# Layer 0 of a two-layer graph kernel on one core: source keys through DRAM instead of by broadcast transposes, two more one-hot tiles for two fewer gathers, and the ranks cut into pieces

## The chip, the cores and the metric

The kernel runs on one core of one Trainium2 chip. The metric is the device time of the whole kernel in microseconds (us), the median of several runs. TensorE is called PE here, VectorE DVE, ScalarE ACT, GpSimd POOL and SyncE SP, as the profile does.

## The reference, cut to what matters

There are 12,500 nodes with 32 features and 400,000 edges, sorted by `dst`. Two layers are applied to `x`:

```python
h = relu(layernorm(x))                                   # layer 0
agg = segment_sum((h * node_vec1)[src], dst)             # gather by src, add by dst
x = x + agg * node_vec1_n2
h = relu(layernorm(x))                                   # layer 1
m = relu(h[src] + edge_attr_32)
x = x + (1 + eps) * h + segment_sum(m, dst)
```

All of the change that matters lies in layer 0, the first line pair with its gather by `src`.

## The kernel before

The edges are cut into 125 units of 128 x 25 edges, and these into 25 batches of five units: three "sorted" and two "plain". A batch covers a narrow range of `dst`, so its sums go into a window of PSUM by products with one-hots of the destination. What differs is how the source rows are fetched.

**Sorted units.** DVE works out for each of their edges a place in a table of records that is ordered by source (`rank_within`, `rank_sums`, `rank_places`). POOL scatters the edges there, one indirect DMA of 128 edges at a time, 75 for a batch. A batch's records then come back in one load (`load_record`), as 100 tiles of 128 edges in ten groups, the source key of each edge in column `2 * F` of its record. For each group PE turns the keys of ten tiles into rows, each by a transpose of a column broadcast to 125 partitions (`turn_keys`), ACT copies them from PSUM to `key_row` in two pieces (`copy_keys`), DVE compares them with the partition's number (`src_onehots`), and PE multiplies these one-hots with the node table held in SBUF (`pick`). DVE also makes the one-hots of the destination (`dst_onehots`), and PE adds the messages by them (`products`). This is called the sorted phase of a batch here.

**Plain units.** Their 50 tiles (one from each column) are sorted by source inside each row. Of them, `DIRECTS` = 2 * `SIDE` = 38 are picked by PE from the node table with wide one-hots, in eight steps (`CUTS`, `STEPS`), the node table being met in 20 groups of which a tile needs 3 to 8 (`SPANS`); the remaining 12 (`MID`) are gathered by POOL (`gather_mid`). The eight steps are called the wide phase here, and their steps are numbered 0 to 7. In it, DVE makes the wide one-hots of a step (`wide_onehots`), the sorting of later rows (`sort_some`) and the destinations' one-hots (`direct_onehots`); ACT copies each picked tile masked (`copy_wide`); PE picks (`pick_wide`) and adds (`direct_products`).

**Order.** Each engine has its own hand-written program, in batches, and they meet by semaphores. In the step of batch b, DVE does the rest of the sorted phase of b, then the wide phase of b. Inside or after that wide phase it ranks batch b + 2 (whose scatter POOL begins when `ranked` says so), and then begins the sorted phase of b + 1 with `first_onehots`: the source one-hots of groups 0 and 1, then the destination one-hots of these groups. PE turns the keys of the first two groups of b + 1 in the last tiles of the wide phase of b, as soon as that batch's record is loaded. SP issues all plain loads and stores in program order: a wait in its program holds back everything behind it. The PE, ACT and POOL programs loop over two batches (`over_batches`), those of DVE and SP over four in layer 0 (`over_fours`).

## Time and profile before

| | |
|---|---|
| time, median of 3 runs | 4801.34 us (4799.08 to 4803.71) |
| time of the profiled execution | 4791.23 us |
| its span, first to last instruction | 4789.2 us |
| granted PE clock over it | 0.914 |
| busy: PE, DVE, ACT, POOL | 3721.2, 3812.7, 3261.3, 3497.5 us |

The profile is of one execution. Layer 0 is the time from the start to about 3,060 us, when the last sums are added and x is loaded again, and layer 1 is the rest. Start times are counted from the first instruction. A row of the timeline merges neighbouring instructions of a line, and in brackets it gives the idle time of the engine before them and what ended it.

### The profile page before, as it was taken

The page shows a single profiled execution, that of the slowest core. Times are in us where ns is not written, and L with a number is a line of the kernel's source. Part 1 is how long each engine was busy: PE and PEld are TensorE (multiplying, and loading weights), DVE is VectorE, ACT ScalarE, POOL GpSimd, SP SyncE. Part 2 cuts the span into 40 slices and gives each one's busy share as a digit, 9 for nine tenths or more (in the row PEclk, how much of TensorE's full clock was granted, in tenths as well). Part 3 has the DMA queues.
Part 4 walks back from the last instruction along what each step waited for, and adds up shares of the span by engine and source line. Part 5 has one row for each costly group of instructions (what it writes and reads, how often), then busy time and mean ns, then how long its engine had stood idle before and what let it go on. Part 6 is the DMA issues. An engine that isn't in the chain of part 4 may idle for free.

```text
span 4789.2 us, 130194 instructions
## 1 busy us (share of the span) xinstructions
PE 3721.2 (78%) x43852; PEld 2888.9 (60%) x43852; DVE 3812.7 (80%) x11454; ACT 3261.3 (68%) x9090; POOL 3497.5 (73%) x3590
## 2 busy tenths in 40 slices
PE   0388888888888888888888899467767777777775
PEld 0266666666666666666666666356666666666664
DVE  9788888888888888888888886767777776777775
ACT  1377777777777777777777777456666766666664
POOL 6757777777777777777777777477777777777774
PEclk9999999999999999999999999778888888888887
DMA  6322222222222222222222221211212221211221
GB/s 111 63 51 54 57 54 54 54 56 54 54 54 56 54 53 54 56 54 53 54 56 54 53 54 44 72 39 54 57 43 54 57 57 54 58 49 48 57 57 26
DMA packets 439702, 262.77 MB, mean 55 GB/s; under 512 B 334660, under 2 KB 423732, under 8 KB 432632
## 3 DMA queue, kind: packets, MB, share of 16 engines
q1 hardware_dynamic: 322488, 187.55, 16.7%
q0 software_dynamic: 110816, 60.69, 6.7%
q8 instruction: 394, 6.46, 0.6%
q10 hardware_dynamic: 5728, 5.82, 0.5%
q14 instruction: 276, 2.26, 0.2%
HBM read 172.96 MB, written 80.85 MB: 53 GB/s over the span
## 4 chain that ended last, share of the span: by engine, by line
PE 32%; POOL 23%; DVE 19%; issue 13%; ACT 10%; DMA 2%; DVEq 1%; ACTq 0%; SPq 0%; POOLq 0%
POOL stage L759 22%; PE candidates L1247 18%; PE plain_ps L1259 7%; DVE arena L1753 7%; ACT message L987 5%; DVE arena L1729 4%; ACT centered L956 2%; PE sorted_agg L1187 2%; PE candidates L1157 1%; ACT arena L880 1%; POOL message L759 1%; PE key_rows L1230 1%; DMA stage<-in_edge_attr 1%; DVE counts L1475 1%; PE key_rows L1139 1%
## 5 line engine op out<-in xcount | busy, mean ns | idle before, releaser
L771 POOL DMA_INDIRECT records<-stage,place_i x1875 | 1879.0, 1002 | 696.2 <-issue 652.0
L759 POOL DMA_INDIRECT stage<-table,src_plain x1250 | 1246.9, 997 | 409.1 <-issue 377.3
L987 ACT ACTIVATE message<-candidates,member_is 128x96 bf16<-128x96 f32 x4560 | 1170.7, 377 | 429.4 <-PE candidates L1247 426.3
L1753 DVE TENSOR_SCALAR arena<-window_iota,dst_rel 128x224 bf16<-128x224 f16 (+1 forms) x4800 | 1091.2, 302 | 37.8
L880 ACT ACTIVATE arena<-key_rows 125x640 f16<-125x640 f16 x1000 | 653.2, 716 | 215.1 <-DVE arena L1729 83.2
L1187 PE MATMUL sorted_agg<-arena 128*96 128x224 bf16 (+1 forms) x5000 | 654.1, 285 | 161.0 <-DVE arena L1753 109.6
L1259 PE MATMUL plain_ps<-summed,message 128*96 128x224 bf16 x4560 | 609.2, 269 | 68.2 <-ACT message L987 68.2
L1187 PEld LDWEIGHTS sorted_agg<-arena 128*96 128x96 bf16 x5000 | 543.7, 137 | 186.1 <-issue 118.6
L1259 PEld LDWEIGHTS plain_ps<-summed,message 128*96 128x96 bf16 x4560 | 490.7, 128 | 269.6 <-ACT message L987 127.4
L1729 DVE TENSOR_SCALAR arena<-arena,row_key 125x1280 bf16<-125x1280 f16 x1000 | 554.7, 555 | 96.5 <-ACT arena L880 64.6
L1139 PE MATMUL key_rows<-ident,record 128*125 128x128 f16 x5000 | 425.8, 235 | 239.2 <-DMA record<-records 96.2
L1139 PEld LDWEIGHTS key_rows<-ident,record 128*125 128x125 f16 x5000 | 378.5, 149 | 285.9 <-issue 148.3
L1165 PE MATMUL candidates<-record,ident 128*128 128x320 f32 x500 | 240.0, 568 | 389.8 <-DVE arena L1729 389.3
L1247 PE MATMUL candidates<-parts,xs 125*128 125x480 bf16 x2304 | 526.1, 366 | 0.0
L1170 PEld LDWEIGHTS candidates<-parts,arena 125*128 125x128 bf16 x15000 | 427.0, 99 | 85.4 <-issue 70.9
L1247 PE MATMUL candidates<-parts,record 125*128 125x480 bf16 x1992 | 457.4, 367 | 0.0
L1170 PE MATMUL candidates<-parts,arena 125*128 125x32 bf16 x15000 | 425.8, 180 | 0.0
L1039 ACT ACTIVATE centered<-window_iota,plain_key 128x128 bf16<-128x128 f16 x1250 | 379.9, 391 | 26.3 <-DVE plain_key L1792 25.7
L752 POOL DMA_INDIRECT message<-table,mid_src x288 | 306.4, 1064 | 93.2 <-issue 93.2
L896 ACT ACTIVATE arena<-candidates 128x320 bf16<-128x320 f32 x250 | 108.5, 434 | 368.2 <-PE sorted_agg L1187 363.4
L888 ACT ACTIVATE arena<-candidates 128x480 bf16<-128x480 f32 x500 | 264.6, 584 | 134.0 <-PE candidates L1157 133.3
L1247 PE MATMUL candidates<-parts,arena 125*128 125x480 bf16 x1512 | 341.9, 366 | 0.0
(228 smaller groups left out, 5139.0 us busy)
## 6 DMA issues: line engine op xcount, KB each, us to landing
record<-records SPq DMA_DIRECT2D x50, 1650.0 KB
stage<-in_edge_attr SPq DMA_DIRECT2D x125, 400.0 KB, 3.2
records<-pad SPq DMA_DIRECT2D x25, 1650.0 KB, 11.9
records<-stage,place_i POOLq DMA_INDIRECT x1875
stage<-table,src_plain POOLq DMA_INDIRECT x1250
message<-table,mid_src POOLq DMA_INDIRECT x288
xs<-in_x SPq DMA_DIRECT2D x8, 390.6 KB
table<-parts ACTq DMA_DIRECT2D x4, 585.9 KB
```

The source lines that it names most:

```text
L759: pool.indirect_dma_start(message[:, k, j, :] if l == 0 else rows[:, k, j, :], None, table0 if l == 0 else table1, bass.IndirectOffsetOnAx ...
L771: pool.indirect_dma_start(records, bass.IndirectOffsetOnAxis(ap=place_i[:, h, e:e + 1], axis=0), stage[:, h, e, :], None).then_inc(scatter ...
L880: nc.scalar.activation(key_row[:, g % 2, k * HALF * P:(k + 1) * HALF * P], key_rows[k][0:NP, 0:HALF * P], ACT.Copy).then_inc(key_rows_copi ...
L987: last = nc.scalar.activation(direct_message[n % DB][:, m * WIDE:(m + 1) * WIDE], candidates[n % 2][:, m * WIDE:(m + 1) * WIDE], ACT.Copy, ...
L1039: last = nc.scalar.activation(plain_onehot[:, k, j, :], window_iota[:, 0:WS], ACT.Abs, bias=plain_key[:, k, j:j + 1], scale=-1.0)
L1139: last = nc.tensor.transpose(key_rows[k][0:NP, t * P:(t + 1) * P], column, ident16[:])
L1170: last = nc.tensor.matmul(candidates[g % 2][:, tile * F:(tile + 1) * F], src_onehot[:, g % 2, o, tile * P:(tile + 1) * P], parts[:, 2 * bu ...
L1187: last = nc.tensor.matmul(into, sorted_message[:, (2 * h + g) % MESSAGES, t, :], dst_onehot(g, t), start=(g == 0 and t == 0), stop=(g == G ...
L1247: last = nc.tensor.matmul(candidates[n % 2][:, 0:MEMBERS * WIDE], wide_onehot(s, w)[:, i * P:(i + 1) * P], parts[:, w * MEMBERS:(w + 1) * ...
L1259: last = nc.tensor.matmul(pair_agg, direct_message[n % DB][:, m * WIDE:(m + 1) * WIDE], direct_onehot[:, n % DO, :], start=(n == 0 and m = ...
L1729: nc.vector.tensor_scalar(src_onehot[:, g % 2, o, :], key_row[:, g % 2, :], row_key[0:NP, o:o + 1], None, ALU.is_equal).then_inc(src_oneho ...
L1753: last = nc.vector.tensor_scalar(dst_onehot(g, t), window_iota[:, 0:WA if tile == 0 else WT], dst_rel[:, h, tile:tile + 1], None, ALU.is_e ...
```

## The change

It has four parts, all in layer 0. (Some semaphores of the far path are merged as well, which has no part in a run on these inputs, since that path is only taken when an edge lies outside its window.)

- **Keys.** PE turns the keys of a whole batch by one transpose, 128 x 100 to 100 x 128 (`turn_all`), ACT copies it to SBUF (`copy_turned`), SP stores it to a DRAM tensor `turned`, waits for that, and loads it back group by group, 1280 keys broadcast to 125 partitions, into four buffers (`key_of`); from the fifth group on a load waits until the one-hots four groups before it are made. These stand in SP's program between the record's load and the loads of the stage and the filling of batch b + 2. `copy_keys` and `turn_keys` are gone from layer 0.
- **Tiles.** `SIDE` goes from 19 to 20: 40 of 50 plain tiles are made by one-hots, 10 gathered. Steps 3 and 4 have five tiles instead of four.
- **Ranks.** `rank_within` is cut in two: `rank_buckets` in step 2 of the wide phase and a third of the scans (`rank_scans`) in each of steps 2, 3 and 4, instead of everything at step 5.
- **Places.** `rank_sums` and `rank_places` move from behind the wide phase to the end of step 6, ahead of the one-hots of step 7; PE's `prefixes` moves from step 6 to step 5.

```diff
-    SIDE = 19
+    SIDE = 20
-    CUTS = (0, 5, 10, 15, 19)
+    CUTS = (0, 5, 10, 15, 20)
+    turned = nc.dram_tensor("turned", (BATCHES, TILES * P), F16, kind="Internal").ap()
+        def key_of(l, g):
+            return more_rows[:, g % 2, :] if l == 0 and g % KEY_ROOMS >= 2 else key_row[:, g % 2, :]
...
@@ SP, step0, behind load_record(0, b, 0)
+                if is_first(b):
+                    sp_at_least(parts_ready, CHUNKS)
+                sp.wait_ge(key_rows_copied[0], b + 1)
+                sp.sem_inc(loads_begun, 1)
+                sp.dma_start(turned_t[bass.ds(b, 1), :, :].rearrange("o t e -> (o t) e"), keys_turned[:]).then_inc(keys_stored, 16)
+                sp.wait_ge(keys_stored, 16 * (b + 1))
+                sp.sem_inc(loads_begun, 1)
+                for g in range(GROUPS):
+                    nth = GROUPS * b + g
+                    if g == 0:
+                        sp_at_least(src_onehot_ready[0], 2 * GROUPS * b)
+                    elif g >= KEY_ROOMS:
+                        sp_at_least(src_onehot_ready[0], 2 * (nth - KEY_ROOMS + 1))
+                    sp.dma_start(key_of(0, g), turned_g[bass.ds(nth, 1), :].to_broadcast([NP, GE])).then_inc(keys_loaded[g % KEY_ROOMS], 16)
                 if left >= 2:
                     load_stage(b + 2, h)
                     fill(b + 2, h)
@@ ACT
+                def copy_turned(b):
+                    act.wait_ge(key_rows_ready[0], b + 1)
+                    at_least(act, keys_stored, 16 * b)
+                    nc.scalar.activation(keys_turned[:], key_rows[0][0:TILES, 0:P], ACT.Copy).then_inc(key_rows_copied[0], 1)
...
-                            if n in (DIRECTS - 3, DIRECTS - 2):
-                                copy_keys(*after(b, h, u), n - (DIRECTS - 3))
+                            if n == DIRECTS - 3:
+                                copy_turned(b + 1)
@@ PE
+                def turn_all(b):
+                    pe.wait_ge(record_loaded[0][0], 16 * (b + 1))
+                    at_least(pe, direct_copied_keys, SUBS * b)
+                    nc.tensor.transpose(key_rows[0][0:TILES, 0:P], record16[:, 0, :, 2 * F], ident16[:]).then_inc(key_rows_ready[0], 1)
...
-                            if n in (DIRECTS - 3, DIRECTS - 2):
-                                turn_keys(*after(b, h, u), n - (DIRECTS - 3))
+                            if n == DIRECTS - 3:
+                                turn_all(b + 1)
@@ DVE, step0, at the end of step s of the wide phase
-                            if s == SUBS - 3 and more:
-                                rank_within(b + 2, h, u + 1)
-                        if more:
-                            rank_sums(b + 2)
-                            rank_places(b + 2, h, u + 1)
+                            if s == 2 and more:
+                                rank_buckets(b + 2, h, u + 1)
+                            if s in (2, 3, 4) and more:
+                                rank_scans(b + 2, s - 2)
+                            if s == SUBS - 2 and more:
+                                rank_sums(b + 2)
+                                rank_places(b + 2, h, u + 1)
                         first_onehots(*after(b, h, u))
```

How the end of a wide phase and the start of the next sorted phase stand in DVE's program, before (`record<-direct_row` is step 6, `xs<-direct_row` step 7, `summed` their destination one-hots, `counts` the rank sums, `key<-unhandled` the last of the places, and the row of line 1729 the source one-hots of groups 0 and 1):

```order
L1808 TENSOR_SCALAR record<-direct_row,wide_key 125x640 x8
...
L1819 TENSOR_SCALAR summed<-window_iota,pair_dst 128x224 x5
L1808 TENSOR_SCALAR xs<-direct_row,wide_key 125x640 x5
L1819 TENSOR_SCALAR summed<-window_iota,pair_dst 128x224 x5
L1475 TENSOR_TENSOR counts<-counts,misc 128x1250 x3
L1478 TENSOR_TENSOR counts<-counts,in_bucket 128x3750
...
L1516 TENSOR_SCALAR key<-unhandled 128x75
L1729 TENSOR_SCALAR arena<-arena,row_key 125x1280 x4
L1742 CAST dst_rel<-record 128x100
```

And of the change:

```order
L1853 TENSOR_SCALAR record<-direct_row,wide_key 125x640 x8
...
L1864 TENSOR_SCALAR summed<-window_iota,pair_dst 128x224 x5
L1516 TENSOR_TENSOR counts<-counts,misc 128x1250 x3
L1519 TENSOR_TENSOR counts<-counts,in_bucket 128x3750
...
L1557 TENSOR_SCALAR key<-unhandled 128x75
L1853 TENSOR_SCALAR xs<-direct_row,wide_key 125x640 x5
L1864 TENSOR_SCALAR summed<-window_iota,pair_dst 128x224 x5
L1774 TENSOR_SCALAR arena<-arena,row_key 125x1280 x4
L1787 CAST dst_rel<-record 128x100
```

The rank sums and places now stand ahead of step 7's one-hots, so that nothing but two short rows lies between step 7's one-hots and the source one-hots of the next batch.

SP's program between the record's load and the stage's, of the change, with its waits (`turned` is the DRAM tensor of the turned keys, `arena` and `centered` hold the four buffers; the six later loads follow as the last two rows do, each with a wait for the one-hots):

```order
L603 DMA record<-records 128x3300
L650 ISA [waits key_rows_copied0]
L650 DMA turned<-keys_turned 100x128
L651 REGISTER_ALU
L586 REGISTER_ALU [waits keys_stored]
L659 ISA [waits src_onehot_ready0]
L659 DMA arena<-turned 125x1280
L659 ISA
L659 DMA arena<-turned 125x1280
L659 ISA
L659 DMA centered<-turned 125x1280
```

Before, the record's load was followed at once by the stage's:

```order
L594 DMA record<-records 128x3300
L586 ISA
L586 DMA stage<-in_edge_attr 128x25x32
L586 ISA
L586 DMA stage<-in_edge_attr 128x25x32
L586 ISA
L586 DMA stage<-in_edge_attr 128x25x32
```

So a store, a wait for it and ten loads of 125 x 1280 keys now lie in SP's program ahead of the stage's loads.

## Rows read from the trace of the kernel before

**Rows 1.** POOL's groups of lines from 1162.37 to 2107.21 us, eight batches

```profile
L771 POOL DMA_INDIRECT records<-stage,place_i x600 | 600.2, 1000 | 213.8 <-issue 209.4 <-DVE key L1516 4.4
L752 POOL DMA_INDIRECT message<-table,mid_src x96 | 102.2, 1064 | 29.3 <-issue 29.3
```

**Rows 2.** DVE's timeline: wide phases of batches 2, 9, 10, 11, 22 begin

```profile
454.05 1.09 DVE L1808 TENSOR_SCALAR record<-direct_row,wide_key 125x640 bf16<-125x640 f16 x3
...
1277.19 1.33 DVE L1808 TENSOR_SCALAR record<-direct_row,wide_key 125x640 bf16<-125x640 f16 x3
...
1397.86 1.24 DVE L1808 TENSOR_SCALAR record<-direct_row,wide_key 125x640 bf16<-125x640 f16 x3
...
1514.83 0.67 DVE L1808 TENSOR_SCALAR record<-direct_row,wide_key 125x640 bf16<-125x640 f16 x2
...
2810.01 1.15 DVE L1808 TENSOR_SCALAR record<-direct_row,wide_key 125x640 bf16<-125x640 f16 x3
```

**Rows 3.** DVE's timeline behind the wide phase of batch 9

```profile
1355.43 1.14 DVE L1729 TENSOR_SCALAR arena<-arena,row_key 125x1280 bf16<-125x1280 f16 x2
...
1368.35 1.14 DVE L1729 TENSOR_SCALAR arena<-arena,row_key 125x1280 bf16<-125x1280 f16 x2 [4.47 <-ACT arena L880]
1371.05 1.15 DVE L1729 TENSOR_SCALAR arena<-arena,row_key 125x1280 bf16<-125x1280 f16 x2 [1.55 <-ACT arena L880]
```

**Rows 4.** DVE's timeline in and behind the wide phase of batch 10

```profile
1431.45 3.49 DVE L1808 TENSOR_SCALAR xs<-direct_row,wide_key 125x640 bf16<-125x640 f16 x9 [1.96 <-ACT direct_row L949]
...
1460.49 1.81 DVE L1808 TENSOR_SCALAR xs<-direct_row,wide_key 125x640 bf16<-125x640 f16 x5
1462.33 1.28 DVE L1819 TENSOR_SCALAR summed<-window_iota,pair_dst 128x224 bf16<-128x224 f16 x5
...
1478.13 1.14 DVE L1729 TENSOR_SCALAR arena<-arena,row_key 125x1280 bf16<-125x1280 f16 x2
...
1488.03 1.14 DVE L1729 TENSOR_SCALAR arena<-arena,row_key 125x1280 bf16<-125x1280 f16 x2 [0.52 <-ACT arena L880]
```

**Rows 5.** DVE's groups by shape, 1162.37 to 2107.21 us

```profile
L1819 DVE TENSOR_SCALAR summed<-window_iota,pair_dst 128x224 bf16<-128x224 f16 x304 | 79.5, 311 | 20.0 <-PE plain_ps L1259 4.5 <-DVE member_is L1711 1.9 <-issue 0.4
...
L1808 DVE TENSOR_SCALAR record<-direct_row,wide_key 125x640 bf16<-125x640 f16 x105 | 38.1, 400 | 1.4
...
L1808 DVE TENSOR_SCALAR record<-direct_row,wide_key 125x512 bf16<-125x512 f16 x72 | 24.1, 371 | 1.1
```

**Rows 6.** PE's timeline, a full tile and the end of the wide phase

```profile
1366.03 1.22 PE L1139 MATMUL key_rows<-ident,record 128*125 128x128 f16 x9 [4.49 <-issue]
...
1425.54 1.79 PE L1247 MATMUL candidates<-parts,xs 125*128 125x480 bf16 x8
...
1427.64 1.58 PE L1247 MATMUL candidates<-parts,xs 125*128 125x480 bf16 x7
...
1467.98 1.18 PE L1247 MATMUL candidates<-parts,xs 125*128 125x480 bf16 x5
...
1471.84 0.34 PE L1139 MATMUL key_rows<-ident,record 128*125 128x128 f16 x3
...
1479.52 0.70 PE L1157 MATMUL candidates<-parts,arena 125*128 125x96 bf16 x7 [3.87 <-DVE arena L1729]
```

**Rows 7.** SP's timeline: a store, a load behind its landing

```profile
1459.19 0.38 SPq L647 DMA_DIRECT2D ordered<-row_order  x1
1461.13 0.40 SPq L650 DMA_DIRECT2D row_order<-ordered  x1
```

**Rows 8.** ACT's timeline: first keys copied

```profile
1473.17 1.32 ACT L880 ACTIVATE arena<-key_rows 125x640 f16<-125x640 f16 x2
```

**Rows 9.** DMA issues of the page: KB each, us to landing

```profile
stage<-in_edge_attr SPq DMA_DIRECT2D x125, 400.0 KB, 3.2
```

**Rows 10.** Windows: the last two numbers are DMA share and GB/s

```profile
2989.00:2990.00 1.00, 1.00 (x9) 0.58 (x8) 0.00 (x0) 1.00 (x5) 0.94 (x1) 1.00 1.00 422
...
3104.00:3105.00 1.00, 0.00 (x0) 0.00 (x0) 1.00 (x2) 0.00 (x0) 0.00 (x0) 0.50 0.32 128
```

More of the change, by code:

```diff
@@ L401, in gnn_two_layers @@
         key_rows_copied = per_layer("key_rows_copied")
+        keys_stored = sem("keys_stored")
+        keys_loaded = [sem(f"keys_loaded_{k}") for k in range(KEY_ROOMS)]
         src_onehot_ready = per_layer("src_onehot_ready")
@@ L1429, in rank_within, with rank_buckets @@
             def rank_within(b, h, u):
+                rank_buckets(b, h, u)
+                for v in range(SORTED):
+                    rank_scans(b, v)
+            def rank_buckets(b, h, u):
                 nth = [0]
@@ L1449, in rank_within, with rank_scans, step @@
                         bucket16[:, v * J:(v + 1) * J].unsqueeze(1).to_broadcast([P, BUCKETS, J]), ALU.is_equal))
[L1450 to L1457 removed]
+                assert nth[0] == 8 + SORTED
+            def rank_scans(b, v):
+                nth = [8 + SORTED + v * len(SCANS)]
+                def step(ins):
+                    nth[0] += 1
+                    ins.then_inc(rank1_steps, 1)
+                    dve.wait_ge(rank1_steps, b * RANK1 + nth[0])
+                for some in SCANS:
+                    last = nc.vector.tensor_tensor_scan(counts[:, v, some], goes_on[:, 0:some.stop - some.start],
+                                                        in_bucket[:, v, some], 0.0, ALU.mult, ALU.add)
+                    if v < SORTED - 1 or some != SCANS[-1]:
+                        step(last)
+                if v == SORTED - 1:
+                    last.then_inc(scans_ready, 1)
+                    assert nth[0] == RANK1
             HALVINGS = []
```

59 lines of the change are left out of this document (26 added, 33 removed).

## Prediction

> **What bounds the kernel now.** The change touches layer 0 alone, so I read the groups of lines of eight batches first, to see which engine is always occupied, and then the timelines of DVE and PE over one wide phase and what follows it.
>
> POOL looks like the bound and is nearly so. A scatter takes 1.00 us and the next starts 0.30 us later, so the 75 of a batch are 97.9 us, and the 12 gathers are (102.2 + 29.3) / 8 = 16.4 us: 114.3 us in each batch [rows 1]. The batches take longer than that: DVE starts the wide phase of batch 2 at 454.05 and that of batch 22 at 2810.01, which is 117.8 us each [rows 2]. POOL waits the difference, for the ranks. So the cycle is made by DVE and PE.
>
> That cycle has two parts, cut at the first source one-hots of the next batch (called src0 below). In batch 9, W, the start of the wide phase, is at 1277.19, src0 at 1355.43 (W + 78.2), and the next W 42.4 us later. In batch 10: W at 1397.86, src0 at 1478.13 (W + 80.3), and the next W 36.7 us later [rows 2 to 4]. The sum over the two is 237.6 us. In the wide phase PE and DVE run side by side. PE starts step 7 at W + 70.1 and turns the next keys at W + 74.0; then it waits 3.87 us for src0, because DVE is still in the ranks [rows 6]. In the sorted phase DVE runs with hardly a gap in batch 10 (0.52 us for keys), while in batch 9 it waits 4.47 + 1.55 us for them [rows 3, 4], which comes from a pause of 4.49 us on PE that nothing in the profile explains [rows 6]; it comes at every second batch, where PE's program starts its loop again. So the keys' transposes and copies are beside the path in one batch of two.
>
> **What is taken off.** (1) Ninety-nine transposes and nineteen copies of a batch. In the sorted phase DVE does the same one-hots as before, so all that can be won is its wait for keys: 0.5 us in batch 10. In batch 9 the 6.0 us shrink: groups 2's keys no longer come through PE, but group 3's one-hots still wait for the second pick, which stands behind PE's pause. Counting from src0: the first pick and four products end at 6.1 as before (1366.03 - 4.49 - 1355.43), the pause at 10.6, the pick some 1.5 later, and DVE would be ready for group 3 at about 11 (1488.03 - 0.52 - 1478.13, and 1.4 of (7)); some 1.5 us stay. So 4.5 us are won there. (2) Two gathers: POOL's floor falls by 2.7 to 111.6 us, worth nothing while it isn't the bound. (3) Ranks in pieces: DVE does the same work at other moments. At step 5 it waited 1.96 us for its keys because it was ahead of PE [rows 4]; with the ranks earlier it won't be. That is 2.0 us less on DVE's way to src0 (I use it for both batches).
>
> **What is added.** (4) Two tiles that need 8 node groups each. From one 8-group tile to the next PE takes 2.10 us [rows 6], so 4.2 us, less 0.2 for two gathered tiles: PE reaches step 7 at W + 74.1. DVE gets two more destination one-hots of 79.5 / 304 = 0.26 us and 18 wide one-hots widened from 512 to 640, by 0.363 - 0.335 = 0.03 us each [rows 5]: 1.0 us.
>
> (5) Places sooner. The 1.85 us and 1.28 us of step 7 [rows 4] now come behind the ranks. DVE would start step 7 at W + 80.3 - 2.0 - 3.1 + 1.0 = W + 76.2 in batch 10, with the first pair of one-hots 0.75 us later (two of five in 1.81) at 76.9; in batch 9 at 74.9. PE wants them at 74.1, so PE now waits 0.8 to 2.8 us at step 7, which it never did. What POOL gains (its scatter may start some 3 us sooner) it doesn't need.
>
> (6) The new way of the keys, which is the main cost. PE turns them behind the third tile of step 7, 3.86 us after its start (1471.84 - 1467.98, [rows 6]), and 0.3 more because the first tile has to wait for its last one-hots: W + 81.1 in batch 10, 79.1 in batch 9. From there to src0:
> - ACT's copy began 1.33 us after the turn's start [rows 6, 8], as it finishes a tile first; with a copy of 0.3 us: 1.6. SP's reaction: 0.2.
> - The store, and the wait for it. The nearest pair, also a store to DRAM whose landing lets a load go, takes 1461.13 - 1459.19 = 1.94 us [rows 7].
> - The load. A load of 400 KB lands in 3.2 us [rows 9]. Data at full speed moves at 422 GB/s with a DMA share of 1.00; so 1.0 us of it is data and 2.2 us are fixed. But a transfer on 125 partitions, the store of the node table, runs at a share of 0.32 and 128 GB/s [rows 10]: five engines of sixteen. The key load writes 125 x 2560 B = 320 KB on 125 partitions, so 2.5 us, and lands after 4.7 us.
>
> In sum 8.4 us, all of it on the path: DVE has nothing left in its program between step 7 and src0 that could cover it, and from W + 79 on it is idle. Before, the keys were turned and copied while DVE was in 14.5 us of ranks. src0 comes at 81.1 + 8.4 = W + 89.5 in batch 10 and W + 87.5 in batch 9, that is 9.2 us later in both.
>
> (7) The second key load lands 2.5 us behind the first and DVE wants it after 1.1: 1.4 us more. Later groups are wanted every 3.4 us ((1514.83 - 1488.03) / 8, [rows 2, 4]), so a load of 2.5 us keeps ahead, with four buffers.
>
> (8) SP issues the stage's loads some 20 us later than now, behind the key loads. The scatter wants them almost a whole batch later. No cost; were the cover gone, it would be some microseconds of POOL's, which has 5 to spare.
>
> [...]
>
> **Sum.** Batch 10: + 9.2 - 0.5 + 1.4. Batch 9: + 9.2 - 4.5 + 1.4. Together 16.2 us, 8.1 a batch; there are 24 such passages: 194 us. The start adds nothing (DVE is sorting while the first keys travel). The profiled execution took 4791.2 with a span of 4789.2, so 4985; it was 10.1 us below the median of the runs shown, so I expect 4995.
>
> **Bounds.** The keys' way is between 6.4 (3.2 us for the load, ACT free at once) and 11 us (a receipt and load twice as slow to start); PE's wait at step 7 between 0 and 3; the retained part of the pause between 0 and 6. That is 5 to 11 us a batch.
>
> **Rivals.**
> - *All sixteen engines carry the keys.* Nothing in the trace shows a broadcast read from DRAM on 125 partitions. At 422 GB/s 320 KB take 0.8 us: src0 1.7 us earlier, no second wait: 8.1 - 3.1 = 5.0 us a batch, 4921. Against it is the share of 0.32 [rows 10]. With all shades up to 6 us: chance 0.22.
> - *The broadcast reads are slow*, 125 reads of the same 2560 B. At half the speed a load takes 5 us, more than the 3.4 us in which DVE uses one up. The first keys come 2.5 us later, and the tenth load lands 45 us behind the first where DVE wants it about 31 us after src0: 2.5 + 14 more, 24 us a batch, about 5380. It turns from a few us to this at 3.4 us a load. Chance 0.06, and 0.10 for something between.
> - *The keys are there before DVE wants them* (faster). Then DVE's own work sets the pace: 2.0 less and 1.0 more in the wide phase, 0.5 and 4.5 us fewer waits in the sorted one: 3.5 us a batch, from the pair's 118.8 down to 115.3, above POOL's 111.6: 4717. It decides where the way from the turn to src0 is under 2 us. The store and its wait alone took 1.94. Or PE's and ACT's lighter load shortens the wide phase by more than I see. Chance 0.05.
> - *Nothing changes*, because POOL sets the pace: against it are 3.5 us a batch of waiting. Chance 0.02.
> - My forecast, 6 to 10 us a batch: 0.55.
>
> Differences under 0.2%, some 10 us, are what a measurement of this kernel can't tell from none. The range 4895 to 5085 leaves out the ends of both sides.
>
> **What would show it.** DVE's row of the source one-hots at the head of each batch has an idle time of 8 to 11 us, ended by a DMA of `turned`; the second one has 1 to 2 us; the store and the first load stand some 2 us apart in SP's rows; the loads run at a share near 0.31; PE waits for DVE's `xs` one-hots at step 7; POOL waits 9 to 12 us a batch for ranks; the period is 125 to 127 us. Wrong would be a short wait there, which would mean the keys' way costs under 5 us, or sorted phases longer than 40 us with waits at every group, which would be slow loads.

## The result and the profile after

The changed kernel takes 5037.8 us (median of four runs, 5032.0 to 5040.0) beside 4802.3 for the kernel before (four runs, 4799.1 to 4803.7): ratio 1.049, 95% interval 1.0471 to 1.0508. That is 235 us more, or 9.8 us for each of the 24 passages from one batch to the next. I had forecast 8.1 a batch, so 4995 us, with a range of 4895 to 5085.

First the page of the kernel after, engines, and the groups of POOL's scatters and of DVE's source one-hots:

```profile
PE 3704.0 (74%) x42001; PEld 2824.8 (56%) x42001; DVE 3831.8 (76%) x11502; ACT 3041.6 (60%) x8807; POOL 3433.4 (68%) x3542
...
L794 POOL DMA_INDIRECT records<-stage,place_i x1875 | 1877.5, 1001 | 994.1 <-issue 765.6
...
L1774 DVE TENSOR_SCALAR arena<-arena,row_key 125x1280 bf16<-125x1280 f16 x800 | 447.1, 559 | 346.5 <-DMA arena<-turned 330.7
```

PE and DVE are busy for about as long as before (3704 and 3832 us beside 3721 and 3813); it is idle time that has been added. In front of the source one-hots 330.7 us of it are ended by the key loads, which alone is more than the 235 us lost. POOL's groups of lines over eight batches (1246.98 to 2270.12 us), the answer to [rows 1], show who follows and doesn't lead:

```profile
L794 POOL DMA_INDIRECT records<-stage,place_i x601 | 598.3, 995 | 322.6 <-issue 257.5 <-DVE key L1557 65.1
L775 POOL DMA_INDIRECT message<-table,mid_src x80 | 78.6, 983 | 24.4 <-issue 24.4
```

Between two scatters POOL idles 0.30 us, which makes 180 of these 322.6 us. The other 142 us, some 18 a batch, are one long wait in each batch, until the ranks are there. In every second batch the profile puts it down to them (65.1 us), in the others, where the wait stands at the same place in the batch, to "issue". Worked out in the same way, the kernel before has 4 us a batch of such waits [rows 1].

DVE's timeline around the passage from batch 9 to batch 10 (start, duration; in brackets the idle time before and what ended it), the answer to [rows 2 to 4]:

```profile
1372.11 2.04 DVE L1853 TENSOR_SCALAR record<-direct_row,wide_key 125x640 bf16<-125x640 f16 x5
...
1445.71 0.20 DVE L1557 TENSOR_SCALAR key<-unhandled 128x75 f32 x1
1445.90 1.82 DVE L1853 TENSOR_SCALAR xs<-direct_row,wide_key 125x640 bf16<-125x640 f16 x5
1447.84 1.33 DVE L1864 TENSOR_SCALAR summed<-window_iota,pair_dst 128x224 bf16<-128x224 f16 x5
1461.12 1.14 DVE L1774 TENSOR_SCALAR arena<-arena,row_key 125x1280 bf16<-125x1280 f16 x2 [11.95 <-DMA arena<-turned]
1463.89 1.35 DVE L1774 TENSOR_SCALAR arena<-arena,row_key 125x1280 bf16<-125x1280 f16 x2 [1.62 <-DMA arena<-turned]
...
1475.99 2.43 DVE L1774 TENSOR_SCALAR arena<-centered,row_key 125x1280 bf16<-125x1280 f16 x4 [5.24 <-issue]
...
1504.09 2.04 DVE L1853 TENSOR_SCALAR record<-direct_row,wide_key 125x640 bf16<-125x640 f16 x5
```

With W = 1372.11, step 7's one-hots start at W + 73.8, and the source one-hots, which follow them in DVE's program, only at W + 89.0: DVE has been idle for 11.95 us and then for 1.62 more. The 5.24 us further down belong to every fourth batch (5.0 to 5.2 us in batches 5, 9, 13 and 17). PE's timeline in the same place:

```profile
1446.63 1.51 PE L1277 MATMUL candidates<-parts,xs 125*128 125x480 bf16 x5 [1.08 <-DVE xs L1853]
...
1450.84 0.22 PE L1170 MATMUL key_rows<-ident,record 128*100 128x128 f16 x1
...
1462.49 1.78 PE L1187 MATMUL candidates<-parts,arena 125*128 125x96 bf16 x20 [9.35 <-DVE arena L1774]
...
1468.49 1.02 PE L1187 MATMUL candidates<-parts,arena 125*128 125x96 bf16 x20 [1.15 <-issue]
```

PE waits 1.08 us for the one-hots of step 7, turns the keys at W + 78.7 and then waits 9.35 us, where it had waited 3.87 [rows 6]. Between the turn and the source one-hots stand ACT's copy, the store and the loads; ACT's and SP's timelines:

```profile
1452.17 0.30 ACT L909 ACTIVATE keys_turned<-key_rows 100x128 f16<-100x128 f16 x1
```

```profile
1452.70 0.35 SPq L650 DMA_DIRECT2D turned<-keys_turned  x1
1455.05 0.75 SPq L659 DMA_DIRECT2D arena<-turned  x2
1456.00 0.72 SPq L659 DMA_DIRECT2D centered<-turned  x2
```

From the turn to the copy 1.33 us, to the store 0.53, to the first load 2.35, to the one-hots 6.07: 10.3 us. And windows of one microsecond (the last three numbers: granted PE clock, DMA share, GB/s):

```profile
1457.00:1458.00 1.00, 0.00 (x0) 0.00 (x0) 0.00 (x0) 0.00 (x0) 0.95 (x1) 0.50 0.40 81
1458.00:1459.00 1.00, 0.00 (x0) 0.00 (x0) 0.00 (x0) 0.00 (x0) 0.70 (x2) 0.50 0.35 78
1459.00:1460.00 1.00, 0.00 (x0) 0.00 (x0) 0.00 (x0) 0.00 (x0) 0.69 (x2) 0.50 0.38 76
1460.00:1461.00 1.00, 0.00 (x0) 0.00 (x0) 0.00 (x0) 0.00 (x0) 0.70 (x2) 0.50 0.32 115
1461.00:1462.00 1.00, 0.00 (x0) 0.00 (x0) 0.84 (x2) 0.00 (x0) 0.80 (x1) 0.50 0.39 141
```

The DMA share is about 0.38, in which other transfers have a part, and the core's DMA moves only some 80 GB/s in the first microseconds of the burst and 141 later. The queue of the key loads by itself has 30.3% of the sixteen engines' time from 1456 to 1468 us, which is five engines of sixteen (4.8).

The tables below give means over the twenty batches 2 to 21, read as just done, from the first wide one-hots of a batch (W) to those of the next. "Turn" is the start of PE's (first) key transpose, "idle" DVE's idle time right before the first source one-hots, src0 their start, "sorted" the time from there to the next W, all in us. A period comes from the one execution that was profiled; the difference of two median times, divided by 24, comes within 0.7 us of the difference of the two periods.

| kernel | turn | idle | src0 | sorted | period |
|---|---|---|---|---|---|
| before | 74.2 | 0.06 | 79.1 | 38.7 | 117.8 |
| after | 78.9 | 11.6 | 88.8 | 38.8 | 127.6 |

All that was lost lies ahead of src0: 9.8 us.

### The profile page after: what moved, and what is told of

Its sections match the earlier page's. It is cut to its first block, busy times and chain, and to the rows that moved or that the text cites. A ratio compares the mean times of both kernels' runs of the same rounds, so it can differ in the third digit from the quotient of the medians.

```text
span 5037.0 us, 127139 instructions
## 1 busy us (share of the span) xinstructions
PE 3704.0 (74%) x42001; PEld 2824.8 (56%) x42001; DVE 3831.8 (76%) x11502; ACT 3041.6 (60%) x8807; POOL 3433.4 (68%) x3542
## 4 chain that ended last, share of the span: by engine, by line
DVE 34%; POOL 22%; PE 16%; issue 16%; DMA 7%; ACT 4%; DVEq 1%; SPq 0%; ACTq 0%; POOLq 0%
POOL stage L782 21%; PE candidates L1277 10%; DVE arena L1798 9%; DVE arena L1774 5%; DMA arena<-turned 4%; PE plain_ps L1289 3%; DVE counts L1492 2%; ACT message L1015 2%; DVE counts L1516 2%; DVE record L1853 2%; DVE summed L1864 1%; DVE xs L1853 1%; DVE counts L1524 1%; PE sorted_agg L1217 1%; DVE row_order L1696 1%
## 5 line engine op out<-in xcount | busy, mean ns | idle before, releaser
L1015 ACT ACTIVATE message<-candidates,member_is 128x96 bf16<-128x96 f32 x4800 | 1232.8, 369 | 500.2 <-PE candidates L1277 494.4
L1774 DVE TENSOR_SCALAR arena<-arena,row_key 125x1280 bf16<-125x1280 f16 x800 | 447.1, 559 | 346.5 <-DMA arena<-turned 330.7
L1289 PE MATMUL plain_ps<-summed,message 128*96 128x224 bf16 x4800 | 642.3, 269 | 56.2 <-ACT message L1015 56.2
L1187 PE MATMUL candidates<-parts,arena 125*128 125x96 bf16 x5000 | 297.7, 223 | 331.2 <-DVE arena L1774 310.3
L1277 PE MATMUL candidates<-parts,record 125*128 125x480 bf16 x2184 | 498.6, 366 | 0.0
L1200 PEld LDWEIGHTS candidates<-parts,arena 125*128 125x128 bf16 x15000 | 424.8, 98 | 93.1 <-issue 78.6
L1187 PEld LDWEIGHTS candidates<-parts,arena 125*128 125x128 bf16 x5000 | 271.2, 108 | 359.6 <-issue 295.4
L1277 PE MATMUL candidates<-parts,arena 125*128 125x480 bf16 x1704 | 384.7, 365 | 0.0
L903 ACT ACTIVATE arena<-key_rows 125x640 f16<-125x640 f16 x500 | 321.4, 695 | 95.1 <-DVE arena L1774 83.3
L1277 PEld LDWEIGHTS candidates<-parts,xs 125*128 125x128 bf16 x2304 | 216.5, 98 | 240.3 <-DVE xs L1853 46.5
L1195 PEld LDWEIGHTS candidates<-record,ident 128*128 128x128 f32 x500 | 91.1, 228 | 411.1 <-DVE arena L1774 277.5
```

Of the source, the lines that this page charges most:

```text
L1015: last = nc.scalar.activation(direct_message[n % DB][:, m * WIDE:(m + 1) * WIDE], candidates[n % 2][:, m * WIDE:(m + 1) * WIDE], ACT.Copy, ...
L1187: last = nc.tensor.matmul(candidates[k][:, t * WIDE:(t + 1) * WIDE], src_onehot[:, g % 2, o, tile * P:(tile + 1) * P], parts[:, 2 * bucket ...
L1195: nc.tensor.matmul(candidates[g % 2][:, 0:GROUP * F], ident[:], record[:, h, g * GROUP:(g + 1) * GROUP, 0:F], start=True, stop=False)
L1200: last = nc.tensor.matmul(candidates[g % 2][:, tile * F:(tile + 1) * F], src_onehot[:, g % 2, o, tile * P:(tile + 1) * P], parts[:, 2 * bu ...
L1277: last = nc.tensor.matmul(candidates[n % 2][:, 0:MEMBERS * WIDE], wide_onehot(s, w)[:, i * P:(i + 1) * P], parts[:, w * MEMBERS:(w + 1) * ...
L1289: last = nc.tensor.matmul(pair_agg, direct_message[n % DB][:, m * WIDE:(m + 1) * WIDE], direct_onehot[:, n % DO, :], start=(n == 0 and m = ...
```

## The experiments

Twelve kernels, the overview first (times in us), then each with its expectation.

| kernel | ratio to before, interval | turn | idle | src0 | sorted | period |
|---|---|---|---|---|---|---|
| keys only | 1.0197, 1.018 to 1.0214 | 74.1 | 4.7 | 83.6 | 38.8 | 122.4 |
| tiles and ranks, no keys | 1.0206, 1.0186 to 1.0225 | 79.3 | 4.8 | 82.2 | 39.6 | 121.8 |
| wide load | 1.0291, 1.0273 to 1.0309 | 79.1 | 9.7 | 86.9 | 37.3 | 124.2 |
| early turn | 1.0094, 1.0077 to 1.0111 | 71.6 | 3.6 | 80.9 | 39.0 | 119.8 |
| tiles only | 1.0152, 1.0136 to 1.0168 | 77.5 | 0.15 | 82.4 | 38.0 | 120.4 |
| ranks only | 1.023, 1.0214 to 1.0246 | 79.5 | 5.8 | 82.3 | 40.2 | 122.5 |
| earlier turn, wide load | 0.99, 0.9884 to 0.9916 | 70.4 | 0.19 | 77.6 | 37.8 | 115.3 |
| the same, places late | 1.0076, 1.0062 to 1.009 | 71.4 | 0.10 | 82.4 | 36.9 | 119.2 |
| earlier turn, narrow load | 1.0016, 1.0004 to 1.0028 | 70.2 | 1.9 | 79.2 | 39.0 | 118.1 |
| earlier turn, wide load, 38 tiles | 0.9871, 0.985 to 0.9892 | 67.4 | 0.0 | 76.5 | 39.0 | 115.5 |
| old rows | one run, 5029.4 us | 78.9 | 11.6 | 88.7 | 38.9 | 127.6 |
| own rows | one run, 5021.0 us | 78.9 | 11.3 | 88.5 | 38.6 | 127.1 |

### Which part costs: keys only, and everything but the keys

The changed kernel with tiles and ranks as before:

```diff
-    SIDE = 20
+    SIDE = 19
-    CUTS = (0, 5, 10, 15, 20)
+    CUTS = (0, 5, 10, 15, 19)
...
-                            if n == FIRST[SUBS - 3] and left_after(b) >= 2:
+                            if n == FIRST[SUBS - 2] and left_after(b) >= 2:
                                 prefixes(b + 2)
...
-                            if s == 2 and more:
-                                rank_buckets(b + 2, h, u + 1)
-                            if s in (2, 3, 4) and more:
-                                rank_scans(b + 2, s - 2)
-                            if s == SUBS - 2 and more:
-                                rank_sums(b + 2)
-                                rank_places(b + 2, h, u + 1)
+                            if s == SUBS - 3 and more:
+                                rank_within(b + 2, h, u + 1)
+                        if more:
+                            rank_sums(b + 2)
+                            rank_places(b + 2, h, u + 1)
```

> Only the keys go the new way (one transpose, store, wait, ten broadcast loads); 19 tiles a side and the ranks as before. My theory, that the way of the keys is the cost and its length is fixed: PE turns at about W + 74 as before, the keys need 9.9 us from there (the length in the changed kernel), so the first source one-hots come at W + 84 instead of 79, idle 5 us behind the ranks; the second load's wait of 1.6 us comes on top, and the sorted phase gives 1.5 back: 5 us a batch, about 4925 us. Rival, that the tiles and the moved ranks are the cost and the keys are hidden: 4790 to 4805.

Measured: 4905.2 us beside 4809.8, 4.6 us a batch by the periods and 4.0 by the times. Rows of DVE and SP, batch 9 to 10:

```profile
1404.80 0.20 DVE L1557 TENSOR_SCALAR key<-unhandled 128x75 f32 x1
1410.26 1.29 DVE L1774 TENSOR_SCALAR arena<-arena,row_key 125x1280 bf16<-125x1280 f16 x2 [5.26 <-DMA arena<-turned]
```

```profile
1402.59 0.35 SPq L650 DMA_DIRECT2D turned<-keys_turned  x1
1404.38 0.75 SPq L659 DMA_DIRECT2D arena<-turned  x2
```

Here the places still stand behind step 7, so about half of the keys' way lies under them, and the wait is 4.7 us instead of 11.6.

The opposite, the kernel before with 40 tiles, ranks in pieces and places sooner, but keys by PE and ACT as before (the two diffs of the next section together):

> Twenty tiles a side, ranks in pieces and places sooner, but the keys by transposes and copies as before. My theory: PE turns at about W + 78.5, 4 us later than before, the first keys are copied 2.6 us later, DVE starts the one-hots at about W + 81 instead of 79: 2 us a batch, about 4850 us. Rival, that these parts are the cost: near 5000 us.

Measured: 4905.3 us, 4.0 a batch and not the 2 or so that I had expected; and with an idle time of 4.8 us before the source one-hots, although the keys have their short way. So neither part is harmless, and the keys' cost and this one (4.6 and 4.0) are 1.2 short of the 9.8 of both (by the times 4.0 and 4.0, 1.8 short): the parts use the same cover.

### The parts of the second half: tiles only, ranks only

The kernel before with two more tiles, nothing else:

```diff
-    SIDE = 19
+    SIDE = 20
-    CUTS = (0, 5, 10, 15, 19)
+    CUTS = (0, 5, 10, 15, 20)
```

> The kernel before with 20 tiles a side (10 gathered) and nothing else. My theory: both tiles lie ahead of PE's turn of the next keys, so the turn moves from W + 74.2 to 78.3, the keys are copied at about 81 and DVE's one-hots start there instead of at 79; their second group waits a us more: 2 us a batch, 4850 to 4860 us. Rival, that two gathers fewer free POOL and pay for the tiles: 4800 or less.

Measured: 4864.9 us beside 4796.4, 2.6 a batch. DVE's group of destination one-hots by shape, 691.31 to 1043.53 us (three batches):

```profile
L1819 DVE TENSOR_SCALAR summed<-window_iota,pair_dst 128x224 bf16<-128x224 f16 x120 | 31.8, 305 | 18.0 <-PE plain_ps L1259 13.1 <-DVE member_is L1711 0.7 <-issue 0.2
```

The kernel before, in the same stretch of time:

```profile
L1819 DVE TENSOR_SCALAR summed<-window_iota,pair_dst 128x224 bf16<-128x224 f16 x114 | 29.7, 307 | 7.0 <-PE plain_ps L1259 1.1 <-DVE member_is L1711 0.7 <-issue 0.2
```

That is 13.1 us of waits for PE's `plain_ps` in some three batches, where the kernel before has 1.1. PE reaches step 7 3.4 us later (two tiles, I had 4.0), and DVE, which can run ahead of it only as far as the buffers go, waits those microseconds for PE and comes to its ranks, and so to src0, 3.3 us later instead of the 1.0 of its own work. So PE paces DVE in the wide phase.

The kernel before with `rank_within` in pieces, places ahead of step 7 and `prefixes` a step sooner, nothing else:

```diff
-                            if n == FIRST[SUBS - 2] and left_after(b) >= 2:
+                            if n == FIRST[SUBS - 3] and left_after(b) >= 2:
                                 prefixes(b + 2)
...
-                            if s == SUBS - 3 and more:
-                                rank_within(b + 2, h, u + 1)
-                        if more:
-                            rank_sums(b + 2)
-                            rank_places(b + 2, h, u + 1)
+                            if s == 2 and more:
+                                rank_buckets(b + 2, h, u + 1)
+                            if s in (2, 3, 4) and more:
+                                rank_scans(b + 2, s - 2)
+                            if s == SUBS - 2 and more:
+                                rank_sums(b + 2)
+                                rank_places(b + 2, h, u + 1)
```

> The kernel before with the ranks in pieces and the places ahead of step 7, 19 tiles a side, keys by transposes. My theory: DVE makes step 7's first one-hots at about W + 75, where PE wants them at 70.3; PE waits 4 to 5 us there, its turn of the keys moves to W + 78.5 and the first source one-hots from 79 to 81.5, with nothing left behind the keys to cover them: 2 to 3 us a batch, 4850 to 4880 us. Rival, that DVE's waits saved at step 5 pay for it: 4760 to 4800.

Measured: 4906.3 us, 4.7 a batch, far over what I had expected; 3.2 of it lie ahead of src0 and 1.5 in the sorted phase. PE's and DVE's timelines, batch 9 to 10:

```profile
1400.46 1.70 PE L1247 MATMUL candidates<-parts,xs 125*128 125x480 bf16 x5 [3.77 <-DVE xs L1822]
...
1406.28 0.74 PE L1139 MATMUL key_rows<-ident,record 128*125 128x128 f16 x10
```

```profile
1399.72 1.82 DVE L1822 TENSOR_SCALAR xs<-direct_row,wide_key 125x640 bf16<-125x640 f16 x5
1401.58 1.42 DVE L1833 TENSOR_SCALAR summed<-window_iota,pair_dst 128x224 bf16<-128x224 f16 x5
1409.06 1.14 DVE L1743 TENSOR_SCALAR arena<-arena,row_key 125x1280 bf16<-125x1280 f16 x2 [6.06 <-ACT arena L880]
```

PE waits 3.77 us for step 7 (3.6 on average), since 14.5 us of places now stand ahead of its one-hots; the turn, which hangs on step 7's third tile, comes 5.3 us later; and DVE has nothing left to do until the keys are there. The turn loses more than PE's wait, because PE is also slower behind it: from the start of step 7 to the turn it takes 5.8 us here (5.5 on average) where it took 3.9. The granted clock is 0.50 from 1401.7 to 1405.0 us, after PE's wait, and 1.00 again from 1405.2. The window (the third number from the end is the granted clock):

```profile
1401.70:1405.00 3.30, 3.30 (x13) 1.98 (x12) 1.23 (x5) 1.27 (x5) 2.39 (x4) 0.50 0.10 20
```

It falls in step 7 in 18 of the twenty batches; in the two where it stays at 1.00, PE takes 4.2 us to the turn. So 1.3 of the 5.3 us are the clock. Even keys that need only a transpose and a copy are late then. So moving the places took the cover from the keys' turn, whatever way the keys take. No kernel has the pieces alone, but PE gets to step 7 at the same time as before (73.9 - 3.6 = 70.3), so the loss begins with the wait for the places. With the two tiles beside it PE's wait is 1.4 us (tiles and ranks), since PE is later by itself: hence 4.0 for both and not 2.6 + 4.7.

### The load: wide, and where it goes slowly

The changed kernel with each key load on 128 partitions:

```diff
-                    sp.dma_start(key_of(0, g), turned_g[bass.ds(nth, 1), :].to_broadcast([NP, GE])).then_inc(keys_loaded[g % KEY_ROOMS], 16)
+                    sp.dma_start(key_room(g), turned_g[bass.ds(nth, 1), :].to_broadcast([P, GE])).then_inc(keys_loaded[g % KEY_ROOMS], 16)
```

(`key_room(g)` is the same buffer as `key_of(0, g)`, on all 128 partitions.)

> The changed kernel with one edit: the key loads are broadcast to 128 partitions instead of 125 (three rows more that nothing reads). If a load on 125 partitions is held to five engines of sixteen, each load gets shorter by some 2 us: the first one-hots come 2 to 3 us earlier and the second ones no longer wait 1.6 us, 3 to 5 us a batch, 4920 to 4965 us, and the DMA share during the loads goes from 0.35 to near 1. Rival, that 125 reads of the same 2560 B are slow whatever the number of engines: no change, 5030 to 5040.

Measured: 4950.9 us, 3.4 a batch less than the changed kernel, made of 1.9 before src0 and 1.4 in the wait before the second one-hots (0.22 instead of 1.66). DVE's row and windows:

```profile
1432.32 2.43 DVE L1780 TENSOR_SCALAR arena<-arena,row_key 125x1280 bf16<-125x1280 f16 x4 [10.13 <-DMA arena<-turned]
```

```profile
1430.00:1431.00 1.00, 0.00 (x0) 0.00 (x0) 0.00 (x0) 0.00 (x0) 0.95 (x1) 0.51 0.93 200
1431.00:1432.00 1.00, 0.00 (x0) 0.00 (x0) 0.00 (x0) 0.00 (x0) 0.69 (x2) 0.50 0.88 330
1432.00:1433.00 1.00, 0.00 (x0) 0.00 (x0) 0.65 (x2) 0.00 (x0) 0.70 (x2) 0.50 1.02 394
```

Three partitions more, whose keys nobody reads, and the share goes from about 0.38 to between 0.88 and 1.02; the loads' own queue goes from 30.3% to 90.8% (1430 to 1433 us). That is the time of 4.8 engines of sixteen beside that of 14.5; why three partitions make this difference, no run shows. But the gain lies on top of a way that stays 7.8 us, and on 128 partitions too the burst starts at half its later speed, 200 beside 394 GB/s.

Two kernels ask where this slow start comes from. The first reads rows written long ago (and so computes wrong messages):

```diff
-                    sp.dma_start(key_of(0, g), turned_g[bass.ds(nth, 1), :].to_broadcast([NP, GE])).then_inc(keys_loaded[g % KEY_ROOMS], 16)
+                    sp.dma_start(key_of(0, g), turned_g[g:g + 1, :].to_broadcast([NP, GE])).then_inc(keys_loaded[g % KEY_ROOMS], 16)
```

> The changed kernel, except that every batch loads the keys of batch 0 from DRAM, long since written, instead of its own; the store and the wait for it stay. (The messages of the later batches are wrong.) What is asked is the way from the first load to the first source one-hots: 6.07 us in the changed kernel, where I had reckoned 4.7, and its first 4 us move 76 to 88 GB/s in packets of 2560 B of about 200 ns, before 132 to 155 GB/s at 102 ns. Theory (the slow start has to do with rows written just before): the load lands in about 4.7 us, the idle time before the first source one-hots falls from 11.6 to about 10.3, the period to some 126.3. Rival (the age of the rows doesn't matter): 11.6 and 127.6 as in the changed kernel, 5035 us.

Measured: nothing moved (idle 11.6, period 127.6). Fresh or old rows make no difference. The second gives each partition other bytes to read, from the node table (its messages are wrong too):

```diff
-                    sp.dma_start(key_of(0, g), turned_g[bass.ds(nth, 1), :].to_broadcast([NP, GE])).then_inc(keys_loaded[g % KEY_ROOMS], 16)
+                    sp.dma_start(key_of(0, g).bitcast(BF16), table0_v.rearrange("p c f -> p (c f)")[:, g % 7 * GE:(g % 7 + 1) * GE]).then_inc(keys_loaded[g % KEY_ROOMS], 16)
```

> The changed kernel, except that the ten loads take, for each of the 125 partitions, 2560 B of its own from the node table in DRAM, instead of one row of 2560 B for all. (The messages are wrong.) Theory (the slow start comes from 125 reads of the same 2560 B, which serve each other slowly until some buffer holds them): packets of 102 ns from the first, idle time before the first source one-hots about 10.3 us instead of 11.6. Rival (it is how any such burst begins after quiet, whatever it reads): the first 4 us again at about 80 GB/s and the idle time 11.6.

Measured: between the two (idle 11.3, period 127.1). Its first load is issued at 1452.73, and the windows are

```profile
1454.00:1455.00 1.00, 0.00 (x0) 0.00 (x0) 0.00 (x0) 0.00 (x0) 0.69 (x2) 0.50 0.26 47
1455.00:1456.00 1.00, 0.00 (x0) 0.00 (x0) 0.00 (x0) 0.00 (x0) 0.90 (x1) 0.50 0.26 73
1456.00:1457.00 1.00, 0.00 (x0) 0.00 (x0) 0.00 (x0) 0.00 (x0) 0.80 (x1) 0.50 0.38 140
```

so full speed is there 3.3 us after the issue and not only after 5 to 6 (the changed kernel has 115 GB/s in its sixth microsecond, 141 in its seventh). The slow stretch is shorter where the rows differ, but the start is slow here as well, and the one-hots gain 0.35 us on average in this one execution. Reading one row for all 125 partitions can explain a part of the slow stretch at most (the rows here come from another tensor too, which no run separates); the rest stays open.

### Can the way be hidden: an earlier turn

The changed kernel with turn and copy two tiles before step 7 instead of three into it:

```diff
-                            if n == DIRECTS - 3:
+                            if n == FIRST[SUBS - 1] - 2:
                                 turn_all(b + 1)
```

(the same at ACT's `copy_turned`)

> The changed kernel with one edit: PE turns the keys, and ACT copies them, four tiles sooner (second last tile but one of step 6 instead of the third of step 7), some 7 us. If it is the length of the keys' way that DVE waits for, the first one-hots come that much sooner, at about W + 82 instead of 89: 6 us a batch, about 4890 us, DVE's wait at the head of a batch 5 us instead of 11.6. Rival, that the wait has another cause (the load's issue, or DMA load from the scatter): less than 2 us a batch, over 4990.

Measured: 4852.3 us, better than the 4890 or so that I had expected. The turn is 7.4 us sooner, src0 8.0, the period 7.8 (I had 6). Nearly every microsecond of the turn arrives at the end, which is what a path looks like. One tile sooner still (`- 3`), together with the wide load:

```diff
-                            if n == FIRST[SUBS - 1] - 2:
+                            if n == FIRST[SUBS - 1] - 3:
                                 turn_all(b + 1)
```

> The changed kernel with the loads on 128 partitions and the turn and copy of the keys five tiles sooner (third last tile of step 6). If the keys' way (7.6 us with these loads) is all that is wrong with the change, the keys are there at W + 77, when DVE is ready for them: first one-hots at W + 77 to 78, sorted phase 37.3 us: 115 us a batch instead of 117.8, 4735 to 4760 us, faster than before. Rival, that the record isn't there yet so early, and PE waits for it with everything behind: 4800 to 4860, with PE idle for the record at the transpose.

Measured: 4748.2 us (4740.2 to 4753.9), 1.0% faster than the kernel before. PE and DVE, batch 9 to 10:

```profile
1335.54 0.30 PE L1176 MATMUL key_rows<-ident,record 128*100 128x128 f16 x1
```

```profile
1337.85 0.20 DVE L1563 TENSOR_SCALAR key<-unhandled 128x75 f32 x1
1338.04 1.82 DVE L1859 TENSOR_SCALAR xs<-direct_row,wide_key 125x640 bf16<-125x640 f16 x5
1339.99 1.33 DVE L1870 TENSOR_SCALAR summed<-window_iota,pair_dst 128x224 bf16<-128x224 f16 x5
1342.41 2.43 DVE L1780 TENSOR_SCALAR arena<-arena,row_key 125x1280 bf16<-125x1280 f16 x4 [1.08 <-DMA arena<-turned]
```

The turn now runs before the places are finished, and a way of 6.9 us (1342.41 - 1335.54) is covered by them and step 7's one-hots but for 1.08 us; in most batches nothing is left (mean 0.19). This is the rival that I had put at 0.05, brought about: 4748 us where I had worked out 4717 for it.

Which of the two edits did it? The same early turn with the load back on 125 partitions (`key_of(0, g)` and `[NP, GE]` as in the changed kernel):

> The run e7_early_wide with the key loads back on 125 partitions (the changed kernel with only the turn and the copy moved ahead, to the third tile before step 7). Theory (the loads on 125 partitions take 2.2 us more each to land, so src0 would wait about 2 us again and the second one-hots 1.5 more, the rest of the way being hidden by the earlier turn): 115.3 + 2 to 4 = 117 to 119 us a batch, 4790 to 4840 us, ratio 0.998 to 1.008. Rival (with the turn this early the ranks hide even the narrow loads, and the 128 partitions were worth nothing in e7): the same as e7, 4740 to 4760, ratio 0.99.

Measured: 4811.7 us, 0.16% over the kernel before and 2.8 a batch over the last one (1.9 us idle at src0 instead of 0.2, 1.9 instead of 0.2 at the second). From the changed kernel's 127.6 the turn's place takes 9.5 us a batch, and the width another 2.8; the gain over the kernel before needs both.

And are the places ahead of step 7 worth anything once the keys are hidden? The fast version with them back behind it (scans still in pieces):

```diff
-                            if s == SUBS - 2 and more:
-                                rank_sums(b + 2)
-                                rank_places(b + 2, h, u + 1)
+                        if more:
+                            rank_sums(b + 2)
+                            rank_places(b + 2, h, u + 1)
```

> As e7, but with the rank sums and places behind step 7 again, as in the kernel before (the scans stay in pieces). If the places ahead of step 7 only cost, by PE's wait for step 7's one-hots, this is 0 to 1.5 us a batch faster than e7 (4710 to 4755), with no wait of PE at step 7. Rival, that POOL needs the places sooner, its cycle being 111.6 us: slower than e7 by 1 to 2 us a batch, with POOL's scatter on the way to the record.

Measured: 4832.0 us, 3.9 a batch slower than with the places ahead, twice what I had given my rival and against my first expectation. DVE, batch 9:

```profile
1357.02 2.22 DVE L1859 TENSOR_SCALAR xs<-direct_row,wide_key 125x640 bf16<-125x640 f16 x5 [4.76 <-PE candidates L1283]
```

With no places in front of it DVE is ready for step 7 at W + 59.3, but its buffer is still being picked by PE: it waits 4.76 us, starts at W + 64.1, and the places come after that wait. Ahead of step 7 they fill it. My rival shows in the trace, but not on the path: at the turn PE now waits for the batch's record, 1.0 us on average, beside 0.1 us with the places ahead. That turn stands at W + 71.4, behind DVE's wait, and at src0 DVE doesn't wait (0.10). So the move that, together with the pieces, costs 4.7 us a batch with the keys' turn behind it is worth 3.9 where the keys are out of its way.

Last, the fast version with 38 tiles and 12 gathers as in the kernel before (`SIDE` = 19 and its `CUTS`):

> The run e7_early_wide with SIDE back at 19, so 38 one-hot tiles and 12 gathers. Theory (once the keys are hidden, the wide phase sets the pace through PE and DVE, and two tiles cost about 3 us of it, as in the tiles alone; POOL's floor of 114.3 us a batch with 12 gathers then comes near): period between POOL's 114.3 and 115.3 - 3, so it is POOL that sets it: 114.3 to 115 us a batch, 4725 to 4745 us, ratio 0.984 to 0.989. Rival (the two tiles are needed, because POOL with 12 gathers would be late with its scatters and the record comes later): slower than e7, 4765 or more.

Measured: 4741.5 us, ratio 0.9871 (0.985 to 0.9892), beside 0.99 (0.9884 to 0.9916) with 40 tiles: the intervals overlap, and the periods in the traces are 115.5 and 115.3. src0 comes 1.0 us sooner and the sorted phase takes 1.2 longer. The two tiles, 2.6 us a batch in the kernel before, neither cost nor bring anything that these runs can tell. What sets the pace now, these runs don't settle: PE waits 2.6 us for step 7's one-hots, DVE 2.5 us a batch for PE's picks in the sorted phase, and POOL has less to spare than ever, since its reckoning of [rows 1] is 114.3 us with 12 gathers. It isn't always busy, though: its long waits are 2.6 us a batch here, and 3.5 with 40 tiles. One more thing stands in the trace. Behind PE's wait the granted clock falls to 0.50 in step 7 in fourteen of the twenty batches, and with 40 tiles in none. The sorted phase takes 38.3 us in the five even batches with such a fall and 36.7 in the five without; with 40 tiles the same two groups of batches have 36.0 and 36.6. So the clock may take back what fewer tiles bring, which no run shows.

## Why the prediction was right, step by step

The direction, the place and the mechanism were right: 9.8 us a batch where I had 8.1 and bounds of 5 to 11. Three terms were off, one of them the other way from the rest, so that the sum is closer than its parts. By its steps:

**(1) The transposes and copies taken off.** This term was too large. I had 5.0 us for the two batches and 1.4 each of (7) against it, so sorted phases shorter by 1.1 us on average; they are as long as before (38.8 beside 38.7). The even batches are 0.9 us longer (37.9 beside 37.0), as forecast. In the odd batches 3, 7 and 11 the saving is there: 38.2, 37.7 and 37.2 us, where the kernel before had 40.9, 40.5 and 41.4. In batches 5, 9, 13 and 17 it isn't: 43.0 us each, with an idle time of 5.0 to 5.2 us on DVE that is put down to no wait. It comes at every fourth batch, and DVE's program starts its loop again every fourth. In the kernel before that pause would have lain under PE's (4.49, [rows 6]); this last is argued from the rows and not shown by a run. Nor is the pause of one length: with the wide load DVE is idle in this place for 3.17 us in batch 5, put down to no wait, and for 2.98 us in batch 9, put down to PE's picks, and PE's own pause, which I had left at 4.5 us, is 1.15 us in batch 9 of the changed kernel (the row of 1468.49). I had counted on DVE no longer standing behind PE's pause, and not asked whether DVE had one of its own beneath it.

**(2) Two gathers fewer**: worth nothing, as said; POOL waited anyway.

**(3), (4), (5) The way to step 7 and to the turn.** PE's own way to step 7 grew by 3.2 us (74.7 - 1.2 - 70.3; forecast 4.0). DVE started step 7 at W + 73.8 and 75.0 in batches 9 and 10, forecast 74.1 and 76.2; PE waited 1.1 and 2.3, forecast 0.8 and 2.8; the turn came at 78.7 and 79.9, forecast 79.1 and 81.1. The last comes 0.8 us sooner than forecast on average. What I missed is in the background: the tiles reach DVE by PE's pace (tiles only, 3.3 us at src0) and not by DVE's own 1.0, and the places' move was itself the removal of a cover (ranks only). The sum came out nearly right because I did add both up to the turn and from there on counted all as path. POOL's waits, of which I made 9 to 12 us a batch, are some 18: the 3.5 of before, the 2.7 of the two gathers and the 9.8 of the longer batch, by my own reckoning 16. They cost nothing here.

**(6) The keys' way**, forecast 8.4, was 9.9 us on average, 10.3 in batch 9. Its start (ACT, SP: 1.8, measured 1.9) was right; the 0.3 us of the copy and the 0.2 of SP in it were my estimates, and batch 9 has 0.30 and 0.23. The store and its wait, 2.35 and in the next batch 2.14 us, were under-sized by 0.2 to 0.4 with the pair of [rows 7] for them. The load was under-sized by 1.4: 6.1 instead of 4.7. I had charged its data at 128 GB/s, the rate of a store that was under way; the first microseconds of this burst run at 76 to 88. src0 came at 89.0 and 89.7, forecast 87.5 and 89.5.

**(7) The second load**: 1.4 forecast, 1.4 measured (1.66 beside 0.24). Later groups never wait for a load, as forecast: all 49 waits of the 330.7 us stand before the first or the second. **(8)** The stage's loads: no wait of POOL for them appears.

In numbers: a turn 0.8 us sooner and a way 1.6 longer than forecast make src0 0.8 later in these two batches (0.6 on average: 9.8 for 9.2), and the sorted phases bring back nothing instead of 1.1: 8.1 + 0.6 + 1.1 = 9.8.

**The rivals.** Sixteen engines: refuted for 125 partitions by the share (30.3%), and its price confirmed by the wide load (3.4 us a batch, worked out 3.1). Slow broadcast reads: in part true, for the first microseconds of each burst alone (76 to 88 GB/s, then 132 to 155), and not for the reason I gave or not for it alone (own rows, too, move 47 and 73 GB/s before their 140); a load later on keeps ahead of DVE. Keys there before DVE wants them: only with the turn moved. Nothing changes: no, POOL only waited longer.

## What to carry to other kernels

The detour through DRAM took about as long wherever it started (where DVE waited for it, 9.0 to 9.9 us on average from the transpose to the source one-hots with loads on 125 partitions, and 7.8 in the wide load), so what decided here was where it started and what work lay over it: the changed kernel lost 4.9% with it behind the last cover, and a version that starts it 8.5 us sooner and loads it on 128 partitions gained 1.0%. A reordering that fills one engine's wait moves everything that hangs on the work pushed back; before moving it, look up what is triggered by that work. And a partition count of 125 beside 128 is worth a look in every load that somebody waits for (its queue had 30.3% of the engines' time here beside 90.8%).

## What the runs showed of the hardware beyond what I expected

- A burst of key loads moves some 80 GB/s for about four microseconds and then 132 to 155 on 125 partitions, and 159 to 200 before 330 to 394 on 128. The age of the rows has no part in it that shows (old rows: 68 to 99 GB/s in the first four, 11.6 us of idle time as with fresh ones). The very first packets are not slow: from 1456.4 to 1457.0 us the core's DMA moves 119 GB/s, and from 1457 to 1460 it moves 78. Why is open.
- A granted PE clock of 0.50 during and after the long wait for the keys: 20 picks take 1.78 us there (1462.49) beside 1.02 at 1.00 (1468.49). Over the span the clock is 0.898 beside 0.914. Here it lies beside DVE's one-hots and costs the path nothing that shows. In "ranks only" it lies on the path, behind a wait of 3.6 us on average, and costs 1.3 us a batch (5.5 us from the start of step 7 to the turn, beside 4.2 where the clock stays at 1.00).
- An idle time of 5.0 to 5.2 us on DVE at every fourth batch of the changed kernel, put down to no wait. Why is open.
